# One-hots of a segment sum made on ScalarE as 1 - |difference|, in place of a comparison on VectorE

## What is computed

```python
# layer 0
h = features @ W_lin.T
basis = gaussian_smearing(edge_distances)
ef = shifted_softplus(basis @ Wf1 + bf1) @ Wf2 + bf2
messages = h[senders] * ef
agg = jax.ops.segment_sum(messages, receivers, num_segments=N_NODES)
return shifted_softplus(agg @ Wm1 + bm1) @ Wm2 + bm2
# layer 1
w = (silu(silu(emb @ mlp_w0 + mlp_b0) @ mlp_w1 + mlp_b1) @ mlp_w2 + mlp_b2).reshape(-1, 4, MUL)
m0 = w[:, 0] * ss
m1 = w[:, 1][:, :, None] * ss[:, :, None] * Y1[:, None, :]
m2 = w[:, 2][:, :, None] * vv
m3 = w[:, 3] * (jnp.einsum('emc,ec->em', vv, Y1) / SQ3)
msg_s = jax.ops.segment_sum(jnp.concatenate([m0, m3], axis=1), receivers, num_segments=num_nodes)
msg_v = jax.ops.segment_sum(jnp.concatenate([m1, m2], axis=1), receivers, num_segments=num_nodes)
```

## Time and profile before

| | |
|---|---|
| median of 3 runs | 2200.56 us (2197.67 to 2209.35) |
| profiled execution | 2202.79 us, of which the span is 2201.0 us |
| PE busy | 1899.1 us, 86% |
| DVE busy | 1370.4 us, 62% |
| ACT busy | 637.9 us, 29% |
| POOL busy | 1569.6 us, 71% |
| mean granted TensorE clock | 0.823 |

### The profile page before, as it was taken

How to read it: one execution, slowest core, us unless ns; L and a number is a source line. 1 busy time by engine, 2 the same in 40 slices (tenths; PEclk the granted TensorE clock), 3 DMA queues, 4 the chain that set the end, 5 groups by cost and what they waited for, 6 DMA issues and landing times.

```text
span 2201.0 us, 34359 instructions
## 1 busy us (share of the span) xinstructions
PE 1899.1 (86%) x10138; PEld 1431.4 (65%) x10138; DVE 1370.4 (62%) x2905; ACT 637.9 (29%) x995; POOL 1569.6 (71%) x1599
## 2 busy tenths in 40 slices
PE   5887877778777887777879999999999999899997
PEld 4665666666666666666557777666776676677766
DVE  6755555555555555555645776666667666666665
ACT  3643343343433433432541111111111111111114
POOL 4777777777777777777147777777777777777770
PEclk8777777777777777777867998898999998988889
DMA  7422222222222222222021111111121221111112
GB/s 217 126 78 78 76 81 76 76 81 76 76 81 76 80 76 76 81 76 62 6 82 51 55 54 53 53 54 54 53 55 54 54 55 54 52 55 54 53 52 66
DMA packets 105683, 152.31 MB, mean 69 GB/s; under 512 B 33982, under 2 KB 65490, under 8 KB 105546
## 3 DMA queue, kind: packets, MB, share of 16 engines
q0 software_dynamic: 50656, 103.11, 17.3%
q1 hardware_dynamic: 54652, 46.76, 7.0%
q10 hardware_dynamic: 336, 2.01, 0.3%
HBM read 138.53 MB, written 13.21 MB: 69 GB/s over the span
## 4 chain that ended last, share of the span: by engine, by line
POOL 68%; issue 22%; PE 7%; DMA 1%; DVE 1%; ACT 1%; SPq 0%; POOLq 0%; DVEq 0%; ACTq 0%
POOL sent L436 68%; DMA unit_in<-in_x 1%; PE bank L984 1%; PE bank L800 1%; PE bank L767 1%; PE bank L815 1%; PE bank L953 1%; PE bank L759 1%; PE bank L988 0%; PE bank L942 0%; PE bank L871 0%; PE bank L879 0%; PE bank L802 0%; DMA sent<-up_table,senders 0%; DMA sent<-h_table,senders 0%
## 5 line engine op out<-in xcount | busy, mean ns | idle before, releaser
L436 POOL DMA_INDIRECT sent<-up_table,senders x784 | 775.3, 989 | 268.2 <-issue 237.7
L436 POOL DMA_INDIRECT sent<-h_table,senders x784 | 766.5, 978 | 263.9 <-issue 238.6
L815 PE MATMUL bank<-onehot,msg 128*128 128x128 f32 x4704 | 794.0, 332 | 7.1 <-DVE sums L1098 4.2
L815 PEld LDWEIGHTS bank<-onehot,msg 128*128 128x128 f32 x4704 | 706.4, 235 | 116.0 <-issue 91.4
L800 PE MATMUL bank<-Wf_sb,hid 128*128 128x128 f32 x1568 | 281.1, 334 | 94.8 <-DVE hid L1114 94.5
L1124 DVE TENSOR_TENSOR msg<-bank,sent 128x512 f32<-128x512 f32 x196 | 135.6, 692 | 349.1 <-issue 189.7
L800 PEld LDWEIGHTS bank<-Wf_sb,hid 128*128 128x128 f32 x1568 | 246.0, 239 | 153.5 <-DVE hid L1114 100.2
L800 PEld LDWEIGHTS bank<-w_sb,h 64*128 64x128 f32 x1568 | 195.5, 193 | 213.1 <-issue 116.2
L631 ACT ACTIVATE soft<-soft 128x512 f32<-128x512 f32 (+1 forms) x209 | 131.2, 628 | 591.2 <-DVE soft L1105 558.4
L1085 DVE TENSOR_TENSOR onehot<-relT,iota 128x512 f32<-128x512 f32 x392 | 268.8, 686 | 39.3 <-PE bank L815 37.1
L800 PE MATMUL bank<-w_sb,h 64*128 64x128 f32 x1568 | 233.9, 291 | 47.3 <-DVE msg L1157 46.4
(11 more groups left out here) (133 smaller groups left out, 1330.4 us busy)
## 6 DMA issues: line engine op xcount, KB each, us to landing
basis<-in_edge_weight SPq DMA_DIRECT2D x196, 100.0 KB
sent<-h_table,senders POOLq DMA_INDIRECT x784
sent<-up_table,senders POOLq DMA_INDIRECT x784, 2.5
basis<-near_lengths SPq DMA_DIRECT2D x196, 16.0 KB
radial_embedding<-basis SPq DMA_DIRECT2D x196, 16.0 KB
emb_in<-radial_embedding SPq DMA_DIRECT2D x98, 32.0 KB
unit_in<-in_x SPq DMA_DIRECT2D x12, 256.0 KB, 3.7
h_table<-h SPq DMA_DIRECT2D x12, 256.0 KB, 2.8
```

Of the source, the lines that this page charges most:

```text
L436: pool.indirect_dma_start(sent[:, n % SLOTS, j, :], None, table, bass.IndirectOffsetOnAxis(pick, 0))\
L815: last = t_.matmul(ps[:, k, :], msg[:, p, j, k * P:(k + 1) * P], onehot[:, p, j, :], start=(j == 0), stop=(j == HALF_CHUNKS - 1))
```

## The change

DVE's one_hots is taken out of both layers. In its place ACT makes the one-hots of a half in five operations: for each of the four chunks |iota - rel| over 128x128 (the function Abs with the chunk's column of -rel as bias) into a new tile `apart`, then one Relu over all 512 columns, 1 - |iota - rel| and not below zero, into the new tile `hot`, which PE reads instead of onehot. The numbers are whole, so the result is exactly one or zero. rel_neg, -rel, is made once by DVE in the setup. ACT calls one_hots for half h - 3 at the end of its step h, so its loops run three steps past the last half. The Abs wait for the Relu before ("hot"), the Relu for the Abs ("apart") and, as `hot` has two buffers, for "window" of two halves earlier. PE's window_sums waits for "hot".

```diff
--- before.py
+++ after.py
@@ -219,6 +219,7 @@
     sums = sb("sums", [P, 2, width])
     scratch = sums[:, 1, :]
     windows_iota = sb("windows_iota", [P, all_windows * WINDOW], I16)
+    rel_neg = sb("rel_neg", [P, pairs, pair_chunks])
     iota = sb("iota", [P, WINDOW])
     ident = sb("ident", [P, P])
     ones = sb("ones", [P, 1])
@@ -271,6 +272,8 @@
     dots = sb("dots", [P, 2, HALF_CHUNKS, 3, MUL])
     dot = sb("dot", [P, 2, HALF_CHUNKS, MUL])
     onehot = sb("onehot", [P, 2, HALF_CHUNKS, WINDOW])
+    apart = sb("apart", [P, HALF_CHUNKS, WINDOW])
+    hot = sb("hot", [P, 2, HALF_CHUNKS, WINDOW])
     emb_in = sb("emb_in", [2 * BESSEL, 2, HALF])
     h1 = sb("h1", [P, 2, HALF])
     h2 = sb("h2", [P, 2, HALF])
@@ -321,6 +324,7 @@
     s_flag, s_fits = sem("s_flag"), sem("s_fits")
     d_emb = sems("d_emb", 2)
     s_norm = sem("s_norm")
+    s_rel = sem("s_rel")
 
     def unit_sems(phase):
 
@@ -347,7 +351,7 @@
         own = (("squared", "basis", "capped", "exped", "logged", "soft"),
                ("act1", "filt2", "act2", "dots", "scaled", "dot"))[layer]
         return by_dma | {k: sem(f"L{layer}_{k}") for k in
-                         ("filt1", "filt", "msg", "window", "added") + own}
+                         ("filt1", "filt", "msg", "window", "added", "apart", "hot") + own}
 
     L0, L1 = edge_sems(0), edge_sems(1)
 
@@ -633,6 +637,22 @@
             a.activation(tile_, tile_, ACT.Ln, scale=0.5, bias=half_const[:, :])\
                 .then_inc(sm[n[1]], 1)
 
+        def one_hots(sm, h):
+
+            p = h.parity
+            b = h.before(2)
+            rel = rel_neg[:, :, :].rearrange("p a b -> p (a b)")
+            b1 = h.before(1)
+            wait(act, sm["hot"], b1.upto())
+            for j in range(HALF_CHUNKS):
+                last = a.activation(apart[:, j, :], iota[:, :], ACT.Abs,
+                                    bias=rel[:, at(h.number(HALF_CHUNKS, j), 1)])
+            last.then_inc(sm["apart"], 1)
+            wait(act, sm["apart"], h.upto())
+            wait(act, sm["window"], b.upto())
+            a.activation(hot[:, p], apart[:, :, :], ACT.Relu, scale=-1.0, bias=ones[:, :])\
+                .then_inc(sm["hot"], 1)
+
         def layer0(h):
 
             if h.parity == 0 and h.real():
@@ -644,8 +664,12 @@
                 act.wait_ge(s_norm, 2)
                 a.activation(norm, norm, ACT.Sqrt).then_inc(s_norm, 1)
                 a.preload_act_table_set("natural_log_exp_and_others")
+            b = h.before(3)
+            if b.real():
+                one_hots(L0, b)
         act.wait_ge(s_weights, 1)
-        for_halves(act, iterations, layer0, 2)
+        act.wait_ge(s_rel, 1)
+        for_halves(act, iterations, layer0, 3)
 
         for nm in (norm0, norm1):
             act.sem_inc(nm["act"], WIDE)
@@ -700,7 +724,10 @@
                     wait(act, L1["filt"], b.upto(3))
                     a.activation(h2[:, g, :], bank[1][:], ACT.Silu, bias=b1_c)\
                         .then_inc(L1["act2"], 1)
-        for_halves(act, iterations, layer1, 0)
+            b = h.before(3)
+            if b.real():
+                one_hots(L1, b)
+        for_halves(act, iterations, layer1, 3)
 
         def finish(back):
             u, r, f = back(0), back(2), back(3)
@@ -807,13 +834,14 @@
 
             p = h.parity
             wait(pe, sm["msg"], h.upto())
+            wait(pe, sm["hot"], h.upto())
             b = h.before(2)
             wait(pe, sm["added"], b.upto())
             ps = winps[p][:, :].rearrange("p (k n) -> p k n", n=WINDOW)
             for k in range(outputs):
                 for j in range(HALF_CHUNKS):
                     last = t_.matmul(ps[:, k, :], msg[:, p, j, k * P:(k + 1) * P],
-                                     onehot[:, p, j, :], start=(j == 0),
+                                     hot[:, p, j, :], start=(j == 0),
                                      stop=(j == HALF_CHUNKS - 1))
             last.then_inc(sm["window"], 1)
 
@@ -1073,20 +1101,11 @@
         for c in range(3):
             copy_turn(dirT[:, :, :, c])
         copy_turn(relT)
+        dve.wait_ge(s_turned, 12)
+        v.tensor_scalar(rel_neg[:, :, :], relT[:, :, :], -1.0, None, ALU.mult).then_inc(s_rel, 1)
         dve.wait_ge(s_flag, 1)
         v.tensor_scalar(sorted_flag[:], bank[6][0:1, 0:1], pairs - 0.5, None, ALU.is_ge)\
             .then_inc(s_flag, 1)
-
-        def one_hots(h, sm):
-
-            p = h.parity
-            b = h.before(2)
-            wait(dve, sm["window"], b.upto())
-            v.tensor_tensor(onehot[:, p],
-                            by_chunk(relT, h).rearrange("p (j a) -> p j a", a=1)
-                            .broadcast_to([P, HALF_CHUNKS, WINDOW]),
-                            iota[:, :].rearrange("p (a n) -> p a n", a=1)
-                            .broadcast_to([P, HALF_CHUNKS, WINDOW]), ALU.is_equal)
 
         def add_window(sm, h, outputs, base):
 
@@ -1207,7 +1226,6 @@
             if b1.real():
                 cap0(b1)
             if b4.real():
-                one_hots(b4, L0)
                 msg0(b4)
             if b6.real():
                 add_window(L0, b6, 1, base)
@@ -1219,7 +1237,6 @@
             if b6.real():
                 add_window(L1, b6, 2, base)
             if b4.real():
-                one_hots(b4, L1)
                 msg1(b4)
 
         def every_window(sm, ev, h, outputs):
```

## The result

The changed kernel takes 2298.46 us in the median of 3 runs (2296.2 to 2298.66) against 2200.56: the ratio is 1.0429, with a 95% interval of 1.0391 to 1.0467. The forecast was 2373 us, in a range of 2225 to 2440: the sign and the ring held, the size was 1.8 times too large (+172 us forecast, +98 measured). The profiled execution took 2296.2 us, 93.4 more than that of before.

A forecast was written before the change was run, and what follows sets the result against it. POOL's pace of issuing gathers was taken to bound the kernel. From 2202.8 us profiled, +198.3 for layer 0's ring, -26.5 for layer 1's shorter gathers, +1 setup, less 2.2 to the median: 2373 us, range 2225 to 2440.

The forecast's parts named there:

- the sign: Whole kernel: the change makes it slower, given a chance of 0.85.
- the ring: Layer 0: PE's window sums, ACT's Relu and basis, then PE's hidden0 wait in a circle; 12.28 us a pair, +198.3 us.
- slow steps: Layer 0, PE: hidden0 through window sums at the lower clock, 6.6 us against 3.63 at full clock, taken for every pair.
- long gap: Layer 0, PE idle over 2 us before hidden0, seven times before the change; forecast 3.1 us every pair, 6.6 us steps following.
- even steps: Layer 0, PE's hidden0, filter0 and window sums in even-numbered loop steps: forecast 6.6 us each.

The follow-up runs named there:

- the longest ring: The changed kernel with a second Relu a half on ScalarE ahead of the real one, into a tile nobody reads: 2450.70 us, 1.1126.
- the shortest: The changed kernel with one Abs a half in place of four, the other three chunks' one-hots left out: 2181.73 us, 0.9889.

## What to carry over

When work moves to another engine, write down what its new place in that engine's order waits for, and what is queued behind it: here 4 us of work a pair cost nothing and a wait one step too young cost 145 us in layer 0. It was enough to place the waiting work one step later, or behind what others wait for, or to give the tile more buffers. Before a cause is read from rows that were picked for it, count the rows that show the same effect without it: 35 slow steps without a long gap stood in the trace of before. And look at what the operation did to its neighbours before moving it: here most of the gain was to be had on the same engine, with the comparison in another form (2157 us), and the best versions, 2148 to 2152 us, keep ScalarE's one-hots and move only the wait.

## What was unexpected in the hardware

- An instruction on a ring through TensorE costs more than its length, by the clock, in the mean over a layer: 1.18 us more of ring a pair made the pair 1.58 us longer, 0.69 us less made it 1.26 us shorter (mean granted clock 0.72, 0.74 and 0.79 from the longest ring to the shortest).
- A slow step of TensorE need not stand behind the longest gap: in the changed kernel even steps behind gaps of 2.33 to 2.46 us took 6.6 us, those behind 3.0 to 3.3 us mostly 5.2 to 6.0.
- Eight idle products in the gap, some 2 us of work, raised the granted clock of layer 0 from 0.74 to 0.98 and took 148 us off the kernel.
- A comparison of two inputs in SBUF lengthens most gathers that start inside it, by 0.3 us on the mean, one against a column of numbers in four shorter instructions by 0.06 us.
